# Far passes behind each engine's code, a hinted image loop and an earlier flag load on TensorE

## The chip, the cores and the metric

The kernel runs on one core of a Trainium2 chip. The metric is the device time of one execution in microseconds (us), taken as the median of three runs. A core has engines that run side by side, each with its own stream of instructions: TensorE (PE in the profile; PEld are its weight loads), VectorE (DVE), ScalarE (ACT), GpSimd (POOL) and SyncE (SP, which starts DMA transfers here). Each has a sequencer that reads the stream, waits for semaphores, works on registers and branches; a q behind an engine's name in a row (PEldq, DVEq, ACTq, POOLq) marks work of the sequencer.

## What is computed

Two blocks with residuals on 32 images of 192 channels and 32 x 32 pixels. The first is attention over channels; the second is a 3 x 3 deformable convolution, batch normalization over all images, and gelu.

```python
x = x + _L0_conv_ref(_gn(x), w_qkv, w_out, b_out)
x = x + _L1_conv_ref(_gn(x), proj_w, proj_b, off_w, off_b, mask_w, mask_b, gamma, beta)
...
offset = jnp.clip(_conv(x, off_w, off_b), -max_off, max_off)
mask = 2.0 * jax.nn.sigmoid(_conv(x, mask_w, mask_b))
y = _deform_conv(x, offset, mask, proj_w, proj_b)
mean = y.mean(axis=(0, 2, 3))
var = y.var(axis=(0, 2, 3))
```

`_deform_conv` takes, for each pixel and each of the nine taps, a bilinear sample of the image at a place shifted by `offset`. The offsets depend on the data, so which rows of the image a pixel reads is known only at run time.

## The kernel before

The program is written by hand, engine by engine, with semaphores between the engines; nothing reorders it. An image's convolution is 48 units (`UNITS`). In unit `u` TensorE turns the sampling weights of unit `u + 2` (`turn_s`, L650), multiplies with those of unit `u` (`convolve`, L667 to L669) and makes a piece of the projected image ten units ahead (`z_group`, L636 to L640). ScalarE and VectorE split each result into a high and a low half (L887 and L1142 for the weights, L853 and L1136 for the projected image). GpSimd builds the sampling weights (L1323). The first block of the next image and its offsets are woven into the same 48 units (`part0`). After unit 47 TensorE transposes the last quarter of the output (`turn_y(3)`, L680 and L681), which VectorE scales (`scale_y(3)`, L1204). With the third `turn_s` of the next image's pass, unit 2 of it begins.

The weights made so reach a few rows only, which is enough while all offsets are small. VectorE therefore finds the image's largest offset and writes a flag `far` for each image. TensorE, ScalarE and VectorE each load it into a register (`is_far`, L387 to L389) and branch on it at the image's end (`where_far`): with flag 1 they run a long `far_pass`, otherwise (a near image) they only count up the semaphores that the far pass would have counted. The code of the far pass stands in the stream at this place, in front of the near code, at four places on each of the three engines. On TensorE one such piece is over 2,000 instructions. In the profiled execution no image was far.

`images` runs image 0 by itself, then a loop over images 1 to 30 whose body holds two images, then image 31 by itself. So of the 31 ends of an image that have another image behind them, 15 lie in the middle of the loop's body, 14 are followed by the jump back to the loop's head (the loop's branch has line L346), one leads from image 0 into the loop and one from image 30 out of it. The loop was opened with `eng.Fori`.

After the last image come the statistics of the batch normalization and a stage that loads, normalizes, adds and stores the images in pairs.

Of the kernel before, what the change touches and what calls it, by code (L numbers as in the profile page):

```python
# [82 lines left out]
def build(nc, x, w_qkT, w_v, w_outT, b_out, w_off, b_off, w_proj, proj_b, gamma, beta,  # L83
          avg, cy, cx, eye, out):
    NB = x.shape[0]
# [4 lines left out]
    with ExitStack() as ctx:  # L90
# [6 lines left out]
        def sem(name):  # L97
            return ctx.enter_context(nc.semaphore(name))
# [166 lines left out]
        far_left = sem("far_left")  # L265
# [63 lines left out]
        def all_pairs(eng, step):  # L329
            with eng.Fori(0, ROUNDS) as r_:  # L330
                for i in range(FIN):
                    step(r_, i)
            for i in range(PAIRS - ROUND_ENDS):
                step(ROUNDS, i)

        def images(program, eng):

            part0, part1, weights_ready = program  # L340
            for u in range(SLOTS):
                part0(u, 0, 0)
                if u == 15:
                    weights_ready()
            part1(0, 0, True)
            with eng.Fori(1, NB - 2, 2) as b:  # L346
                part1(b, 1, True)
                part1(b + 1, 0, True)
            part1(NB - 1, (NB - 1) % 2, False)

        far_units = [(t, ky, f) for t in range(TILES) for ky in range(3)
                     for f, c in enumerate(FAR) if 0 <= t + c <= CHUNKS]
        FAR_UNITS = len(far_units)
# [23 lines left out]
        def first(b):  # L378
            return isinstance(b, int) and b == 0
# [5 lines left out]
        def is_far(eng, b, par):  # L385

            eng.wait_ge(flag_sb, b + 1)  # L387
            eng.sem_inc(flag_seen, 1)
            return eng.value_load(far[0:1, par:par + 1], min_val=0, max_val=1)  # L389

        def where_far(flag, eng, b, par, more, far_pass, *counts):

            with eng.If(flag == 1):
                far_pass(b, par, more)
                eng.sem_inc(far_left, 1)
            with eng.Else():
                for s, n in counts:
                    eng.sem_inc(s, n)

        def load_blocks(eng, dst, src, done):  # L400
            eng.dma_start(dst[:, 0], src[0:P]).then_inc(done, 16)
# [81 lines left out]
        def _(pe):  # L483
# [100 lines left out]
            def offset_max(b):  # L584
                pe.wait_ge(omax_sb, b + 1)
                if not first(b):
                    pe.wait_ge(y_ch, 4 * b)
                pe.transpose(yt[:, 0:P], offmax[:, :].broadcast_to([P, P]), eye32[:, :]).then_inc(omax_ps, 1)

            def part0(u, b, par):  # L590
                if u == 4:
                    group_stats(0, b)
                if 12 <= u < 16:
                    transpose_x(u - 12, b)
                if u == 16:
                    gram_product(b)
                if u == 17:
                    gram_times_wq(b)
                if u == 18:
                    pe.wait_ge(t1_sb, b + 1)  # L600
                    square(log_ps, t1, wk, l0[0], C)
                if u == 21:
                    pe.wait_ge(prob_sb, b + 1)
                    square(r_ps, prob, wo, l0[1], C)
                if u == 22:
                    pe.wait_ge(r_sb, b + 1)
                    for m in range(2):
                        o = l0[0][:, m * C:(m + 1) * C]
                        pe.matmul(o, wv[:, 0, m * P:(m + 1) * P], rmat[:, 0], start=True, stop=False)
                        mm = pe.matmul(o, wv[0:CB, 1, m * P:(m + 1) * P], rmat[0:CB, 1], start=False, stop=True)  # L610
                    mm.then_inc(mt_ps, 1)
                if 23 <= u < 27:
                    apply_m(u - 23, b)
                if u == 28:
                    group_stats(1, b)
                if 38 <= u < 40:
                    for t in range(TILES // 2):
                        offset_conv(TILES // 2 * (u - 38) + t, b, par)

            def z_group(g, b, par):  # L620

                if g == 0:
                    pe.wait_ge(x2_moved, b + 1)
                if g >= 2 or not first(b):
                    pe.wait_ge(z_lo, UNITS * b + g - 1)
                z_product(g, par, par).then_inc(z_ps, 1)
# [15 lines left out]
            def turn_s(u, b):  # L642
                t, ky, c = u // 6, u % 6 // 2, u % 2
                if c == 0:
                    pe.wait_ge(st_made, 24 * b + 3 * t + ky + 1)
                if u >= 2 or not first(b):
                    pe.wait_ge(s_lo, UNITS * b + u - 1)
                g = (3 * t + ky) % ST_RING
                for kx in range(3):
                    mm = pe.transpose(sps[u % 2][:, kx * P:(kx + 1) * P], sT[:, g, kx, c * P:(c + 1) * P], eye32[:, :])  # L650
                mm.then_inc(s_ps, 1)

            def convolve(u, b, par):
                i, ky, c = u // 6, u % 6 // 2, u % 2
                pe.wait_ge(s_lo, UNITS * b + u + 1)
                if i + c < CHUNKS and (c == 1 or i == 0):
                    pe.wait_ge(z_lo, UNITS * b + 6 * (i + c) + 2 * ky + 2)
                if u % 6 == 0 and (i > 0 or not first(b)):
                    pe.wait_ge(y_pm, TILES * b + i)
                s_product(u % S_RING, tile_at(i + c, par), ky, u % 6 == 0, u % 6 == 5).then_inc(sz_done, 1)  # L660
# [11 lines left out]
            def turn_y(q, b):  # L672
                pe.wait_ge(y_pm, TILES * b + 2 * q + 2)
                if q == 0:
                    pe.wait_ge(flag_sb, b + 1)
                if q > 0 or not first(b):
                    pe.wait_ge(y_ch, 4 * b + q)
                for i in range(2):
                    y = ypm[:, (2 * q + i) % 4]
                    pe.transpose(yt[:, i * P:(i + 1) * P], y[:, 0:P], eye32[:, :])  # L680
                    mm = pe.transpose(yt[:, (2 + i) * P:(3 + i) * P], y[:, P:2 * P], eye32[:, :])  # L681
                mm.then_inc(yt_ps, 1)
# [45 lines left out]
            def part1(b, par, more):  # L728
                if first(b):
                    for g in range(AHEAD):  # L730
                        z_group(g, b, par)
                    turn_s(0, b)
                    turn_s(1, b)
                for u in range(UNITS):
                    if u + 2 < UNITS:
                        turn_s(u + 2, b)
                    elif more:
                        turn_s(u + 2 - UNITS, b + 1)
                    convolve(u, b, par)
                    if u == 9:  # L740
                        offset_max(b)
                    if u + AHEAD < UNITS:
                        z_group(u + AHEAD, b, par)
                    elif more:
                        z_group(u + AHEAD - UNITS, b + 1, 1 - par)
                    if u % 12 == 2 and u > 12:
                        turn_y(u // 12 - 1, b)
                    if more:
                        part0(u, b + 1, 1 - par)
                flag = is_far(pe, b, par)  # L750
                turn_y(3, b)
                where_far(flag, pe, b, par, more, far_pass, (fz_ps, FAR_Z), (fs_ps, FAR_UNITS), (fsz_done, FAR_UNITS),
                          (fyt_ps, TILES))

            wq, wk = wqk[:, :, 0:C], wqk[:, :, C:2 * C]
            images((part0, part1, weights_ready), pe)

        @block.scalar
        def _(act):  # L760
# [128 lines left out]
            def part1(b, par, more):  # L889
# [27 lines left out]
                where_far(flag, act, b, par, more, far_pass, (fz_hi, FAR_Z), (fs_hi, FAR_UNITS), (fy_pm, TILES))  # L917

            images((part0, part1, lambda: None), act)

# [7 lines left out]
                                   bias=gb[:, m:m + 1]).then_inc(f_gelu, 1)  # L929

            all_pairs(act, gelu_pair)

        @block.vector
        def _(dve):
# [282 lines left out]
            def part1(b, par, more):  # L1218
# [5 lines left out]
                for u in range(UNITS):  # L1224
# [20 lines left out]
                    if more:  # L1245
                        part0(u, b + 1, 1 - par)
                scale_y(3, b, par)
                where_far(flag, dve, b, par, more, far_pass, (fz_lo, FAR_Z), (f_st, 3 * TILES), (fs_lo, FAR_UNITS),
                          (fy_ch, TILES))
                if not more:  # L1250
                    y_stats(2, b, par)
                    y_stats(3, b, par)

            images((part0, part1, weights_ready), dve)

# [15 lines left out]
                    dve.tensor_tensor(fin_y[slot][i], fin_y[slot][i], fin_x[slot][i], ALU.add).then_inc(f_sum, 1)  # L1272

            all_pairs(dve, add_pair)

        @block.gpsimd
# [112 lines left out]
```

## Time and profile before

| what | value |
|---|---|
| median of 3 runs | 4269.75 us (4259.26 to 4272.78) |
| span of the profiled execution | 4284.4 us |
| PE busy | 3630.2 us, 85% |
| DVE busy | 2649.3 us, 62% |
| ACT busy | 2110.5 us, 49% |
| POOL busy | 1410.9 us, 33% |
| mean granted TensorE clock | 0.939 |

The span is the only time that the profile gives for its own execution; it is 14.65 us above the median of the timed runs. A busy share counts the instructions that compute, not the sequencer's. The granted clock is given as a share of full speed: 1.00 is 2.4 GHz and 0.50 is 1.2 GHz. The images take the span up to some 4050 us, the stage of the pairs the rest.

### The profile page before, as it was taken

What the parts mean: (1) busy time and instruction counts of PE and PEld (TensorE: products, weight loads), DVE (VectorE), ACT (ScalarE), POOL (GpSimd) and SP (SyncE); (2) the same over time, 40 slices, a digit from 0 to 9 for tenths busy, and PEclk for the clock granted to TensorE, in tenths of its full rate; (3) what the DMA queues carried; (4) which work ended last, traced back from release to release, by engine and by line L of the source; (5) the groups of instructions that cost most, each with busy time, mean ns of one, the idle gap of its engine ahead of it and who ended that gap; (6) DMA issues with size and microseconds to landing.
All of it is one profiled execution on the core that took longest, in us unless ns stands there. A gap on an engine that the chain in (4) does not pass through costs nothing.

```text
span 4284.4 us, 109949 instructions
## 1 busy us (share of the span) xinstructions
PE 3630.2 (85%) x38338; PEld 3094.4 (72%) x38338; DVE 2649.3 (62%) x5834; ACT 2110.5 (49%) x4790; POOL 1410.9 (33%) x1165
## 2 busy tenths in 40 slices
PE   3999898999989899998989989898998989899700
PEld 2787777877777778777777877777787777778700
DVE  3666666666666666666666666666666666666522
ACT  1555554555455455545545554554555455445432
POOL 1333332333333233333333333333333333333311
PEclk8999999999999999999999999999999999999955
DMA  2000000000000000000000000000000000000298
GB/s 59 18 27 10 28 27 20 27 27 27 10 27 27 20 27 26 27 10 27 27 20 27 26 27 16 21 27 20 27 26 27 21 16 27 27 20 16 60 361 301
DMA packets 50975, 172.85 MB, mean 40 GB/s; under 512 B 9664, under 2 KB 10880, under 8 KB 50176
## 3 DMA queue, kind: packets, MB, share of 16 engines
q1 hardware_dynamic: 39584, 136.75, 10.6%
q0 software_dynamic: 7168, 25.17, 1.5%
q8 instruction: 426, 6.98, 0.7%
q14 instruction: 373, 3.06, 0.2%
q10 hardware_dynamic: 3424, 0.90, 0.1%
HBM read 87.29 MB, written 75.50 MB: 38 GB/s over the span
## 4 chain that ended last, share of the span: by engine, by line
PE 63%; DVE 13%; issue 13%; ACT 4%; DMA 4%; DVEq 1%; ACTq 1%; SPq 1%; POOL 0%; POOLq 0%
PE sps L650 10%; PE acc L667 6%; PE acc L668 6%; PE acc L669 6%; PE l L578 4%; PE zps L636 3%; DVE zl L1136 3%; PE zps L640 3%; PE zps L637 3%; PE zps L638 3%; PE zps L639 3%; DMA xn<-x_scratch 2%; DVE sl L1142 2%; DVE ych L1204 2%; PE l L510 1%
## 5 line engine op out<-in xcount | busy, mean ns | idle before, releaser
L1323 POOL TENSOR_TENSOR sT<-ay,bx 128x768 f32<-128x768 f32 x768 | 1148.1, 1505 | 1615.3 <-PE sps L650 1547.9
L1142 DVE TENSOR_TENSOR sl<-sps,sh 128x384 f16<-128x384 f32 x1536 | 847.1, 552 | 743.7 <-ACT sh L887 740.3
L887 ACT CAST sh<-sps 128x384 f16<-128x384 f32 x1536 | 741.7, 483 | 915.4 <-PE sps L650 905.9
L667 PE MATMUL acc<-zh,sh 128*128 128x192 f16 x4608 | 1155.7, 251 | 0.3 <-ACT ypm L910 0.3
L668 PE MATMUL acc<-zl,sh 128*128 128x192 f16 x4608 | 1155.5, 251 | 0.0
L669 PE MATMUL acc<-zh,sl 128*128 128x192 f16 x4608 | 1155.2, 251 | 0.0
L650 PE MATMUL sps<-eye,sT 128*128 128x128 f32 x4608 | 808.0, 285 | 322.0 <-issue 218.2
L853 ACT CAST zh<-zps 128x288 f16<-128x288 f32 x1536 | 620.1, 404 | 699.6 <-PE zps L640 672.6
L1136 DVE TENSOR_TENSOR zl<-zps,zh 128x288 f16<-128x288 f32 x1536 | 693.9, 452 | 423.0 <-ACT zh L853 415.7
L650 PEld LDWEIGHTS sps<-eye,sT 128*128 128x128 f32 x4608 | 544.5, 143 | 451.9 <-issue 229.4
L667 PEld LDWEIGHTS acc<-zh,sh 128*128 128x128 f16 x4608 | 459.0, 100 | 37.5 <-issue 35.9
L668 PEld LDWEIGHTS acc<-zl,sh 128*128 128x128 f16 x4608 | 459.1, 100 | 20.9
L669 PEld LDWEIGHTS acc<-zh,sl 128*128 128x128 f16 x4608 | 459.1, 100 | 1.6
L636 PE MATMUL zps<-wpr_h,x_hi_a 128*128 128x288 f16 x1344 | 392.1, 292 | 0.8 <-DVE zl L1136 0.3
L637 PE MATMUL zps<-wpr_l,x_hi_a 128*128 128x288 f16 x1344 | 390.8, 291 | 0.0
L638 PE MATMUL zps<-wpr_h,x_lo_a 128*128 128x288 f16 x1344 | 390.1, 290 | 0.0
L639 PE MATMUL zps<-wpr_h,x_hilo_b 128*128 128x288 f16 x1344 | 389.7, 290 | 0.0
L640 PE MATMUL zps<-wpr_l,x_hilo_b 128*128 128x288 f16 x1344 | 389.7, 290 | 0.0
L1307 POOL TENSOR_TENSOR bx<-off,cx_sb 128x576 f32<-128x576 f32 x128 | 155.3, 1213 | 459.4 <-DVE off L1103 459.4
L1289 POOL TENSOR_TENSOR rstd<-gvar,mhalf 128x2 f32<-128x2 f32 x64 | 44.8, 700 | 582.0 <-DVE gvar L993 582.0
L578 PE MATMUL l<-wof,x2s_hi_a 128*128 128x54 f16 x1536 | 183.0, 186 | 9.8 <-DVE x2w_hilo_b L1009 9.8
L578 PE MATMUL l<-wof,x2s_lo_a 128*128 128x54 f16 x1536 | 182.8, 186 | 0.0
(200 smaller groups left out, 6498.0 us busy)
## 6 DMA issues: line engine op xcount, KB each, us to landing
xin<-in_x SPq DMA_DIRECT2D x32, 512.0 KB, 5.5
xin<-in_x SPq DMA_DIRECT2D x64, 256.0 KB, 5.9
x_scratch<-x SPq DMA_DIRECT2D x32, 512.0 KB, 2.8
y_scratch<-ych SPq DMA_DIRECT2D x32, 512.0 KB, 2.7
zh<-y_scratch SPq DMA_DIRECT2D x20, 512.0 KB, 11.0
zl<-x_scratch SPq DMA_DIRECT2D x20, 512.0 KB, 12.0
out<-zh POOLq DMA_DIRECT2D x20, 512.0 KB, 8.8
x_scratch<-x SPq DMA_DIRECT2D x32, 256.0 KB, 3.5
```

The source lines that it names most:

```text
L578: mm = pe.matmul(o, src[:, row * W:(row + ROWS_T) * W], wof[:, m, k].rearrange("p i j -> p (i j)"), start=(k == 0 and n == 0), stop=(k == ...
L636: pe.matmul(o, at(0), wpr_h[:, 0, ky, n], start=True, stop=False)
L637: pe.matmul(o, at(0), wpr_l[:, 0, ky, n], start=False, stop=False)
L650: mm = pe.transpose(sps[u % 2][:, kx * P:(kx + 1) * P], sT[:, g, kx, c * P:(c + 1) * P], eye32[:, :])
L667: pe.matmul(acc[:, 0:C], s_h, zh[:, j, ky, z], start=start and kx == 0, stop=False)
L668: pe.matmul(acc[:, 0:C], s_h, zl[:, j, ky, z], start=False, stop=False)
L669: mm = pe.matmul(acc[:, 0:C], s_l, zh[:, j, ky, z], start=False, stop=stop and kx == 2)
L853: act.copy(z_piece(zh, g, par), zps[:, g % 2, 0:KO // 2]).then_inc(z_hi, 1)
L887: act.copy(sh[:, u % S_RING].rearrange("p k n -> p (k n)"), sps[u % 2][:, 0:3 * P]).then_inc(s_hi, 1)
L1136: dve.tensor_tensor(z_piece(zl, g, par), zps[:, g % 2, 0:KO // 2], z_piece(zh, g, par), ALU.subtract)\
L1142: dve.tensor_tensor(one(sl), sps[u % 2][:, 0:3 * P], one(sh), ALU.subtract).then_inc(s_lo, 1)
L1323: pool.tensor_tensor(sT[:, p % ST_RING].rearrange("p k (r x) -> p k r x", r=R), a, x_, ALU.mult)\
```

## The change

It has four parts.

- TensorE loads the flag after unit 20's `convolve`, where before it did so behind unit 47.
- Nothing else is moved, and all instructions that compute stay.

```diff
-            with eng.Fori(1, NB - 2, 2) as b:
+            with nc.Fori(1, NB - 2, 2, engines=bass.OrderedEngineSet([eng.engine]), hint_back_edge=True) as b:
...
         def where_far(flag, eng, b, par, more, far_pass, *counts):
 
-            with eng.If(flag == 1):
-                far_pass(b, par, more)
-                eng.sem_inc(far_left, 1)
-            with eng.Else():
-                for s, n in counts:
-                    eng.sem_inc(s, n)
+            k = len(far_bodies)
+            name = f"{eng.engine.name}_{k}"
+            origin = nc.cur_bb
+            eng.br_cond(flag == 1, f"far_{name}", f"near_{name}")
+            nc.switch_bb(f"near_{name}")
+            for s, n in counts:
+                eng.sem_inc(s, n)
+            eng.br(f"joined_{name}")
+            nc.switch_bb(f"joined_{name}", parent=origin)
+            far_bodies.append((name, origin, far_pass, b, par, more))
+
+        def far_code(eng):
+
+            eng.br(f"done_{eng.engine.name}")
+            for name, origin, far_pass, b, par, more in far_bodies:
+                with nc.body(f"far_{name}", parent=origin, valid_engines=[eng.engine]):
+                    far_pass(b, par, more)
+                    eng.sem_inc(far_left, 1)
+                    eng.br(f"joined_{name}")
+            far_bodies.clear()
+            nc.switch_bb(f"done_{eng.engine.name}")
...
                     if u == 9:
                         offset_max(b)
+                    if u == 20:
+                        flag = is_far(pe, b, par)
...
-                flag = is_far(pe, b, par)
                 turn_y(3, b)
...
             images((part0, part1, weights_ready), pe)
+            far_code(pe)
```

On TensorE, at the image's end in the middle of the loop's body, the branch is followed by the far pass before the change (ISA rows are register work and waits, plain semaphore counts are not rows):

```order
L387 REGISTER_ALU
L389 TENSOR_LOAD far
L389 ISA x2
L673 ISA
L677 ISA
L680 MATMUL yt<-eye,ypm 128x128
L681 MATMUL yt<-eye,ypm 128x128
L680 MATMUL yt<-eye,ypm 128x128
L681 MATMUL yt<-eye,ypm 128x128
L393 COMPARE_AND_BRANCH
L685 ISA
```

Over 1,100 rows of far pass later the near code and the next image follow:

```order
L393 UNCONDITIONAL_BRANCH
L396 UNCONDITIONAL_BRANCH
L645 ISA
L647 ISA
L650 MATMUL sps<-eye,sT 128x128 x3
```

After the change the same place reads (all line numbers behind `where_far` are 16 higher here):

```order
L696 MATMUL yt<-eye,ypm 128x128
L697 MATMUL yt<-eye,ypm 128x128
L397 COMPARE_AND_BRANCH
L401 UNCONDITIONAL_BRANCH
L661 ISA
L663 ISA
L666 MATMUL sps<-eye,sT 128x128 x3
```

The far pass and the flag's load are gone from here, and the next image's first `turn_s` stands behind the branch.

On TensorE, at the loop's head, there is one new instruction after the change:

```order
L346 UNCONDITIONAL_BRANCH
L346 BRANCH_PREFETCH_HINT
L346 ISA
L663 ISA
L666 MATMUL sps<-eye,sT 128x128 x3
```

At the loop's end the closing branch now stands two rows behind the flag's branch:

```order
L397 COMPARE_AND_BRANCH
L401 UNCONDITIONAL_BRANCH
L346 REGISTER_ALU
L346 COMPARE_AND_BRANCH
L666 MATMUL sps<-eye,sT 128x128 x3
```

Before, a far pass stood between the two compare-and-branch rows as well.

## Rows read from the trace of the kernel before

**Rows 1.** The page's first part: busy us (share of the span) and instructions.

```profile
PE 3630.2 (85%) x38338; PEld 3094.4 (72%) x38338; DVE 2649.3 (62%) x5834; ACT 2110.5 (49%) x4790; POOL 1410.9 (33%) x1165
```

**Rows 2.** Waits: engine, line, what it waited for: total us, times, longest us.

```profile
PE sps L650 <- issue: 218.2, 46, 8.8
```

**Rows 3.** Timeline of PE, image 1 to 2: start us, us, instruction [idle before].

```profile
361.53 0.68 PE L650 MATMUL sps<-eye,sT 128*128 128x128 f32 x2 [4.34 <-issue]
363.99 0.37 PE L650 MATMUL sps<-eye,sT 128*128 128x128 f32 x1 [1.78 <-issue]
...
369.23 0.49 PE L650 MATMUL sps<-eye,sT 128*128 128x128 f32 x3
...
370.91 0.49 PE L650 MATMUL sps<-eye,sT 128*128 128x128 f32 x3
```

**Rows 4.** Timeline of PE, image 2 to 3, over the loop's jump back.

```profile
488.87 0.90 PE L650 MATMUL sps<-eye,sT 128*128 128x128 f32 x3 [8.53 <-issue]
...
495.00 0.49 PE L650 MATMUL sps<-eye,sT 128*128 128x128 f32 x3
```

**Rows 5.** Timeline of PE, image 0 to 1, then image 30 to 31.

```profile
239.91 0.90 PE L650 MATMUL sps<-eye,sT 128*128 128x128 f32 x3 [4.36 <-issue]
...
245.93 0.49 PE L650 MATMUL sps<-eye,sT 128*128 128x128 f32 x3
...
3972.48 0.73 PE L650 MATMUL sps<-eye,sT 128*128 128x128 f32 x3 [4.25 <-issue]
...
3977.54 0.49 PE L650 MATMUL sps<-eye,sT 128*128 128x128 f32 x3
```

**Rows 6.** Branches by line: count, ns min/median/max, first and last start us.

```profile
L393 PEldq COMPARE_BRANCH  x32: 3435/3771/4165, 234.9 to 4050.7; - x32
...
L346 PEldq COMPARE_BRANCH  x15: 79/4355/4657, 484.3 to 3972.2; - x15
...
L346 POOLq COMPARE_BRANCH  x15: 40/45/50, 469.0 to 3956.8; - x15
```

**Rows 7.** The same view, 354 to 364 us: flag's branch, near code, next image's first instruction.

```profile
L393 PEldq COMPARE_BRANCH  x1: 4022/4022/4022, 356.6 to 356.6; - x1
...
L398 DVEq EVENT_SEMAPHORE  x4: 21/21/21, 360.3 to 360.6; - x4
L398 PEldq EVENT_SEMAPHORE  x4: 51/51/51, 360.7 to 361.2; - x4
...
L645 PEldq FUSED_REGOPS  x1: 51/51/51, 361.3 to 361.3; - x1
```

**Rows 8.** Stretches: us; busy us (instructions) by engine; PEclk, DMA share, GB/s.

```profile
361.40:368.20 6.80, 4.89 (x24) 3.87 (x25) 1.14 (x3) 1.17 (x3) 0.34 (x1) 0.50 0.01 2
368.20:480.00 111.80, 107.62 (x1175) 92.25 (x1174) 76.71 (x174) 62.71 (x146) 41.60 (x34) 1.00 0.09 25
```

**Rows 9.** Timeline of DVE around the same end of image 1.

```profile
358.61 0.98 DVE L1204 TENSOR_SCALAR ych<-yt,unscale,pb 128x256 f32<-128x256 f32 x2
...
370.84 0.54 DVE L1142 TENSOR_TENSOR sl<-sps,sh 128x384 f16<-128x384 f32 x1
371.55 0.46 DVE L1136 TENSOR_TENSOR zl<-zps,zh 128x288 f16<-128x288 f32 x1 [0.17 <-ACT zh L853]
371.92 1.28 DVE L974 BATCH_NORM_STATS2 stats<-xin 128x6 f32<-128x512 f32 x2
...
374.00 0.56 DVE L1142 TENSOR_TENSOR sl<-sps,sh 128x384 f16<-128x384 f32 x1
```

**Rows 10.** Before and behind the flag's load; L680 by form (busy us, mean ns | idle); inside image 2.

```profile
L387 PEldq ALU_OP  x1: 32/32/32, 354.5 to 354.5; - x1
...
L673 PEldq FUSED_REGOPS  x1: 37/37/37, 355.5 to 355.5; - x1
...
L680 PE MATMUL yt<-eye,ypm 128*128 128x128 f32 x256 | 64.5, 279 | 2.9 <-ACT ypm L910 0.5
...
450.02 0.55 PE L650 MATMUL sps<-eye,sT 128*128 128x128 f32 x3 [1.08 <-DVE sl L1142]
```

**Rows 11.** Timeline of DVE behind the last image.

```profile
4054.82 1.28 DVE L1214 BATCH_NORM_STATS2 ystats<-ych 128x6 f32<-128x512 f32 x2 [2.42 <-DVEq L398]
```

## Prediction made before the run

> **What bounds the kernel.** I read the page's busy times first: TensorE is busy for 85% of the span, no other engine for more than 62% [rows 1]. So for the images, which fill nearly all of the span, TensorE's stream sets the pace, and what counts is when it stands still. The view of the waits names one large loss on it: before line L650, which is the turning of the sampling weights, it sat idle for 218.2 us in 46 stretches, and the releaser is "issue": no engine and no DMA was late [rows 2]. The timeline shows where. Each stretch lies at an image's end, behind the last L681. From image 1 to 2, in the middle of the loop's body, PE waits 4.34 us, runs two transposes, and waits another 1.78 us [rows 3]. Over the loop's jump back it waits 8.53 us [rows 4]. Out of image 0 and out of image 30 it waits 4.36 and 4.25 us [rows 5]. The count agrees: 14 ends at 8.5, 17 at 4.25 and 15 second waits of 1.8 make 46 stretches and 119 + 72 + 27 = 218 us.
>
> The sequencer's rows say what it is. The branch on the flag took 3.4 to 4.2 us in all 32 images, always jumping over the far pass to the near code [rows 6]. The loop's branch took 4.36 us at the median, and 79 ns in the one case where it was not taken, at the loop's exit [rows 6]. A jump to code that is far off costs some 4 us, a branch that goes straight on almost nothing. GpSimd's loop branch is taken too, but its body is some 140 instructions, and it took 45 ns [rows 6].
>
> There is a second loss behind each wait. The granted clock is 1.00 in the image (2.4 GHz), and falls to 0.50 (1.2 GHz) for the 6.8 us that follow the wait of image 1 [rows 8]. Since each pause costs twice, I don't add up branches, but measure the whole stretch from the end of the last L681 to the third group of L650, where unit 2 of the next image begins. In full run a unit takes 370.91 - 369.23 = 1.68 us [rows 3], so two units need 3.37 us.
>
> - Middle of the body: 369.23 - (361.53 - 4.34) = 12.04 us [rows 3], 8.67 too long, 15 times.
> - Jump back: 495.00 - (488.87 - 8.53) = 14.66 us [rows 4], 11.29 too long, 14 times.
> - Image 0: 245.93 - 235.55 = 10.38 us; image 30: 3977.54 - 3968.23 = 9.31 us [rows 5]; 7.01 and 5.94 too long.
>
> All of it is 130.1 + 158.1 + 13.0 = 301 us. That is the most that the change can give in the images.
>
> **The change, part by part.**
>
> The branch on the flag. For a near image it is no longer taken, so the nearest row is the loop's exit, 79 ns instead of 3.77 us [rows 6]. The four semaphore counts of the near code stay. They run from 360.7 to 361.2, and the next image's first instruction stands at 361.3 [rows 7]: 0.6 us, and 0.2 more until its first transpose at 361.53 [rows 3]. The branch starts at 356.6 [rows 7], 0.6 us before the last transpose of `turn_y` ends at 357.19, which covers most of it. 0.1 + 0.6 + 0.2 - 0.6 is 0.3, so I take 0.3 us of idle time for PE in the middle of the body. The second wait of 1.78 us, which has the same cause (code behind a jump that isn't there yet), goes too, since nothing is jumped to. The stretch becomes 0.3 + 3.37 = 3.67 us and the gain 12.04 - 3.67 = 8.37 us, 15 times: 125.6 us. Image 30 gains 9.31 - 3.8 = 5.5, and image 0, with a register move and the hint besides, 10.38 - 4.0 = 6.4.
>
> VectorE and ScalarE. VectorE's near code started at 360.3 [rows 7], though its last operation had ended at 359.59 [rows 9]: it pays such a jump too, covered so far by TensorE's longer wait, and loses it in the same way. What is late next is VectorE: it ends `scale_y(3)` at 358.61 + 0.98 = 359.59 us, 2.4 us behind TensorE's last transpose [rows 9]. Then it has for units 0 to 2 a split of the weights, a split of the projected image and a statistic each, then one more statistic and the moments, before TensorE's group sums behind unit 4. A weight split takes 0.54 us, an image split holds the next back by 0.37 (371.55 to 371.92), a statistic adds 0.60 (two take 1.28), and the moments take 0.8, from 373.20 to 374.00 [rows 9]: 3 x 1.51 + 0.6 + 0.8 = 5.9 us, so ready at 365.5. TensorE would be there at 357.19 + 0.3 + 5 x 1.68 = 365.9. It just fits, with 0.4 us to spare, so no loss in the sum, but I allow 0.2 us at each of 31 ends: 6 us back.
>
> The clock. If PE idles for 0.3 to 0.75 us, does it still fall? Inside image 2 PE waits 1.08 us at 450 us [rows 10], and the clock stays at 1.00 from 368.2 to 480 [rows 8]. So I expect no fall, and its share (about 2.5 us at each end, contained in the stretches above) is gained. Its price if it falls nonetheless: 31 x 2.5 = 78 us.
>
> The flag's load in mid-image. The load and the register work around it take TensorE's sequencer from 354.5 to 355.5, about 0.9 us [rows 10]. At the old place the array hardly noticed: the idle time before all 256 transposes of L680, which stand behind it, is 2.9 us [rows 10], since the sequencer works ahead of the array. Ahead of unit 20's `z_group` the mix of instructions is the same, so I cost it at nothing; without that cover it is 0.9 x 32 = 29 us. The flag itself is written in VectorE's unit 11, nine units or 15 us earlier.
>
> The far code behind the rest. At the end each of three engines takes one jump over it, 4 us, when its work is done and the last stores are under way: nothing. VectorE's last branch does lie on the path: its statistics waited 2.42 us [rows 11] for the near code. Gain 2.3 us.
>
> Sum: 125.6 + 147.6 + 6.4 + 5.5 + 2.3 - 6 = 281 us. The profiled span of 4284.4 would become 4003; against the median of 4269.75, 3989 us. Since a run without the profiler may save a little more or less, I put 3990.
>
> **The rivals.**
>
> The hint does nothing (**A**). The jump back still costs one fetch. The nearest row is image 0's end, one jump and the clock behind it, 10.38 us [rows 5]. Each jump back then gains 4.3 instead of 10.54 us, 87 us less in all: 4077 us. For it speaks that the target lies two images of instructions back and that no row shows a hint at work.
> The Trainium skill (Runtime: NRT & Kernel Launch, Instruction fetch mechanics) says that a taken branch whose target is outside the two pages at hand forces a DMA fetch before execution goes on, and names no way round it; the 4.36 us of the loop's branch and GpSimd's 45 ns both agree with that rule. By it the time would be this rival's.
>
> VectorE becomes the bound at the ends (**B**). If the moments or the splits come 1 to 2 us late, through ScalarE's latency or a jump back that VectorE still pays, 31 x 1.5 = 47 us come back: 4036 us. The clock would stay up.
>
> The clock falls in spite of short pauses (**C**): 78 us back, 4068 us.
>
> Slower (**D**): the near code is still jumped to, and its closing branch (L401, unconditional) is a second jump of 3.8 us with 0.5 us more at the low clock. Then each of 31 ends costs 4.3 us more, 133 us, and the hint gives back 14 x 4.3 = 60: 4343 us. It decides on whether a branch to the next address costs a fetch. Against it: the old near code ended in such a branch too (L396), and its last semaphore count and the next instruction stand 0.15 us apart, like the counts among themselves; and the loop's branch has the same form, straight on if false, at 79 ns.
>
> **Chances.** The forecast 0.72; A 0.12; B 0.08; C 0.04; D 0.04. The forecast by itself spans 3968 (nothing of the 301 us stays) to 4018 (the load's 29 us are seen). The range goes from 3968 to 4050, so that B is in; A, C and D are left out, 0.20. This kernel's measurement can tell about 0.3% from no change. Faster by more 0.96, which is the forecast, A, B and C; slower 0.03, and within it 0.01, which share D, since its jumps could cost less where the target is at hand.
>
> **What would show it.** In the changed profile the flag's branch should have some 0.08 us on PE; the loop's branch under 0.5 us; the "issue" wait before `turn_s` should fall from 218 us to under 25; the stretch from the last transpose to unit 2 should be about 3.7 us in the body and 4.1 over the jump; and the granted clock should stay at 1.00 through the images. A loop branch of 4.3 us means A. Waits of `turn_s` or the group sums for VectorE at the ends mean B. A gap in the middle of unit 20 means that the load is not covered. The forecast is wrong if the pauses vanish and the span doesn't follow.

## The result and the profile after

The changed kernel took 3995.86 us (median of 4 runs, 3991.55 to 4003.37), against 4268.81 us before (4 runs here, one more than in the table above): a ratio of 0.9371, 95% interval 0.9349 to 0.9393, or 273 us less. The forecast was 3990 us. The profiled execution had a span of 3992.2 us, 292 us less than the one of before.

The page's first part and its row of the granted clock in 40 slices of the span:

```profile
PE 3544.1 (89%) x38338; PEld 3034.8 (76%) x38338; DVE 2646.4 (66%) x5834; ACT 2111.3 (53%) x4790; POOL 1412.8 (35%) x1165
...
PEclk8999999999999999999999999999999999999955
```

TensorE runs the same 38338 matmuls, but is busy for 86 us less than in [rows 1]. Nothing of its work was taken away, so this is the clock: matmuls at 1.2 GHz last longer. From 120 to 3770 us, which is all of the images but the start of image 0 and the last 2.7 us, the granted clock is 1.00 throughout (columns as in [rows 8]):

```profile
120.00:3770.00 3650.00, 3495.59 (x37896) 3002.51 (x37896) 2540.09 (x5679) 2024.78 (x4694) 1356.28 (x1077) 1.00 0.08 24
```

The same stretch of the kernel before, to 4048 us:

```profile
120.00:4048.00 3928.00, 3579.39 (x37890) 3060.33 (x37889) 2542.46 (x5678) 2023.67 (x4695) 1354.48 (x1077) 0.97 0.08 23
```

The branches on the flag (now L397) and of the loop (L346) on TensorE, columns as in [rows 6]:

```profile
L397 PEldq COMPARE_BRANCH  x32: 71/86/91, 234.7 to 3772.1; - x32
...
L346 PEldq COMPARE_BRANCH  x15: 80/377/404, 465.7 to 3693.4; - x15
```

The flag's branch costs 86 ns instead of 3.77 us (medians). The loop's branch costs 0.38 us instead of 4.36, and 80 ns where it isn't taken.

Of the 218.2 us of waits before `turn_s` in [rows 2] this is left; the first row holds most of the short waits at the images' ends (engine, line, what it waited for: total us, times, longest us):

```profile
PE sps L666 <- POOL sT L1343: 17.3, 23, 1.0
...
PE sps L666 <- issue: 2.7, 8, 0.3
```

That the old waits were for code to be fetched is borne out by the DMA queue that brings TensorE's instructions (queue, kind: packets, MB, share of the 16 DMA engines). Before, then after:

```profile
q8 instruction: 426, 6.98, 0.7%
```

```profile
q8 instruction: 337, 5.52, 0.6%
```

These are packets of 16 KB. In the 13 us around each image's end in the middle of the body (from 1 us ahead of the last transpose's end to 12 us behind it) there were three of them before, and there is one now. The queue is TensorE's: when only the code of ScalarE and VectorE differs (the layout on TensorE alone, below), this row stays at 337, and the other instruction queue, q14, goes from 209 to 347 packets.

The timeline of PE from image 1 to 2, to be held against [rows 3]; L666 is the old L650, and the third row of it opens unit 2:

```profile
350.79 0.54 PE L666 MATMUL sps<-eye,sT 128*128 128x128 f32 x3 [0.33 <-issue]
352.52 0.49 PE L666 MATMUL sps<-eye,sT 128*128 128x128 f32 x3
354.20 0.49 PE L666 MATMUL sps<-eye,sT 128*128 128x128 f32 x3
```

The stretch is 354.20 - 350.46 = 3.74 us, where it was 12.04. Over the jump back from image 2 to 3, against [rows 4]:

```profile
466.47 0.54 PE L666 MATMUL sps<-eye,sT 128*128 128x128 f32 x3 [0.99 <-POOL sT L1343]
...
469.90 0.49 PE L666 MATMUL sps<-eye,sT 128*128 128x128 f32 x3
```

It is 469.90 - 465.48 = 4.42 us, where it was 14.66. The releaser that this row names, GpSimd's weights, is only the semaphore that the instruction looks at. The 0.99 us are filled by the sequencer's own work: the four counts, the counter, 0.40 us of loop branch, the hint and two register instructions stand one behind the other from 465.0 to 466.4.

VectorE behind the last image, against [rows 11]:

```profile
3772.76 0.99 DVE L1223 TENSOR_SCALAR ych<-yt,unscale,pb 128x256 f32<-128x256 f32 x2 [2.34 <-PE yt L697]
3773.78 1.29 DVE L1233 BATCH_NORM_STATS2 ystats<-ych 128x6 f32<-128x512 f32 x2
```

Its statistics follow without the 2.42 us.

The end of the last image's transposes shows how the gain is split. Before and after:

```profile
4051.09 0.27 PE L681 MATMUL yt<-eye,ypm 128*128 128x128 f32 x1
```

```profile
3772.44 0.27 PE L697 MATMUL yt<-eye,ypm 128*128 128x128 f32 x1
```

The images gave 278.65 us. The rest of the span, 233.0 us before and 219.5 after, gave 13.5 more, of which the statistics explain 2.4. The remaining 11 us belong to no edit: the stage of the pairs waits for DMA transfers, and with the same code it lasted from 213.9 to 235.8 us in the profiles of four kernels below that end alike. This is also why the timed runs differ by 273 us where the two profiles differ by 292. For parts worth a few microseconds I therefore read the images' end in the profile, not the total.

### The profile page after: what moved, and what is told of

It is laid out like the page before. It is cut to its first block, busy times and chain, and to the rows that moved or that the text cites. A ratio compares the mean times of both kernels' runs of the same rounds, so it can differ in the third digit from the quotient of the medians.

```text
span 3992.2 us, 110012 instructions
## 1 busy us (share of the span) xinstructions
PE 3544.1 (89%) x38338; PEld 3034.8 (76%) x38338; DVE 2646.4 (66%) x5834; ACT 2111.3 (53%) x4790; POOL 1412.8 (35%) x1165
## 4 chain that ended last, share of the span: by engine, by line
PE 66%; DVE 12%; issue 9%; DMA 4%; POOL 3%; ACT 3%; DVEq 1%; SPq 1%; ACTq 0%; POOLq 0%
PE sps L666 10%; PE acc L683 6%; PE acc L685 6%; PE acc L684 6%; PE l L594 4%; PE zps L652 3%; PE zps L656 3%; PE zps L653 3%; PE zps L655 3%; PE zps L654 3%; DVE zl L1155 3%; DMA xn<-x_scratch 2%; POOL sT L1343 2%; DVE sl L1161 2%; PE l L526 2%
## 5 line engine op out<-in xcount | busy, mean ns | idle before, releaser
L683 PE MATMUL acc<-zh,sh 128*128 128x192 f16 x4608 | 1133.7, 246 | 0.9 <-issue 0.6
L685 PE MATMUL acc<-zh,sl 128*128 128x192 f16 x4608 | 1133.6, 246 | 0.0
L684 PE MATMUL acc<-zl,sh 128*128 128x192 f16 x4608 | 1133.6, 246 | 0.0
L666 PE MATMUL sps<-eye,sT 128*128 128x128 f32 x4608 | 785.8, 279 | 127.2 <-DVE sl L1161 99.4
L666 PEld LDWEIGHTS sps<-eye,sT 128*128 128x128 f32 x4608 | 530.9, 140 | 283.5 <-DVE sl L1161 167.9
L684 PEld LDWEIGHTS acc<-zl,sh 128*128 128x128 f16 x4608 | 450.9, 98 | 17.7 <-issue 0.8
L683 PEld LDWEIGHTS acc<-zh,sh 128*128 128x128 f16 x4608 | 450.8, 98 | 2.4 <-DVE sl L1161 0.5
L685 PEld LDWEIGHTS acc<-zh,sl 128*128 128x128 f16 x4608 | 450.9, 98 | 0.0
```

The lines of the kernel that those rows point to most:

```text
L683: pe.matmul(acc[:, 0:C], s_h, zh[:, j, ky, z], start=start and kx == 0, stop=False)
L684: pe.matmul(acc[:, 0:C], s_h, zl[:, j, ky, z], start=False, stop=False)
L685: mm = pe.matmul(acc[:, 0:C], s_l, zh[:, j, ky, z], start=False, stop=stop and kx == 2)
```

## The experiments

In each timeline below the stretch is measured as in the prediction: from the end of an image's last transpose to unit 2 of the next.

**Without the hint.** The changed kernel, far code behind the rest, no hint.

```diff
-            with nc.Fori(1, NB - 2, 2, engines=bass.OrderedEngineSet([eng.engine]), hint_back_edge=True) as b:
+            with nc.Fori(1, NB - 2, 2, engines=bass.OrderedEngineSet([eng.engine]), hint_back_edge=False) as b:
```

> The changed kernel without the hint on the loop's closing branch; far code stays behind the rest. If the prediction's account of the jump is right (rival A's price), each of the 14 jumps back costs one fetch again: the loop's branch on TensorE takes some 4.3 us, the stretch from the last transpose to unit 2 is some 10.4 us there (3.8 in the body's middle, unchanged), the clock falls behind those 14 alone, and the time is 84 to 88 us above the changed kernel: about 4082 us. If the hint did little and the gain was all in the layout, the time stays within 10 us of 3996.

Measured: 4071.65 us, ratio 0.9526 to the kernel before (0.9507 to 0.9545); against 0.9371 for the change, 66 us more by the two ratios; the images end at 3839.59 us, 67 us later. The loop's branch, the jump back from image 2 to 3, the clock behind it, and TensorE's instruction queue:

```profile
L346 PEldq COMPARE_BRANCH  x15: 67/3649/3829, 464.8 to 3762.1; - x15
```

```profile
468.56 0.55 PE L666 MATMUL sps<-eye,sT 128*128 128x128 f32 x3 [3.97 <-issue]
...
473.64 0.49 PE L666 MATMUL sps<-eye,sT 128*128 128x128 f32 x3
```

```profile
469.50:472.90 3.40, 3.40 (x21) 2.91 (x19) 1.77 (x4) 1.08 (x3) 0.96 (x1) 0.50 0.00 0
```

```profile
q8 instruction: 350, 5.73, 0.6%
```

The jump costs one fetch again, 3.65 us at the median, with 13 packets of code more than in the changed kernel, and the clock falls behind all 14 of these jumps and nowhere else from 120 us to the images' end. So layout and hint are both real: rival A's mechanism exists, and the hint removes it. The stretch is 473.64 - 464.59 = 9.05 us here (9.42 on average over the 14), not 10.4, so the hint's share is 14 x 5.0 = 70 us and not 87. The jump is 0.7 us cheaper than the one of before, and the clock stays low for 3.4 us behind eight of the jumps, where it was 6.8 behind image 0, which I had taken as the nearest row; behind the other six it is 6.8 here too.

The images' end moved by 67 us and not 70 in part because of a wait behind the loop's exit. In the changed kernel TensorE waits in unit 1 of image 31:

```profile
3696.92 0.24 PE L683 MATMUL acc<-zh,sh 128*128 128x192 f16 x1 [0.60 <-issue]
```

Without the hint this wait is absent, and the stretch behind image 30 is 3.83 us instead of 4.62. In the kernels below that have both layout and hint it is 0.87 to 2.91 us, but for the one with 26 counts, which has none. Whether the hint itself or the place of the code makes it was not taken apart.

**The hint alone.** The kernel before, with the hint as the one edit.

```diff
-            with eng.Fori(1, NB - 2, 2) as b:
+            with nc.Fori(1, NB - 2, 2, engines=bass.OrderedEngineSet([eng.engine]), hint_back_edge=True) as b:
```

> The kernel before with the hint alone. Theory: the sequencer fetches the hinted target when it enters the block of code that holds the closing branch. Here it enters that block by the jump to the near code, some 0.7 us ahead of the closing branch, so the fetch has hardly begun: the loop's branch drops from 4.36 to some 3 us at best, and 14 x 1 = 14 us are gained: about 4255 us. Rival (parts add up): the hint is worth the 84 to 88 us by itself, or at least 14 x 4.3 = 60 us: 4209 us or less.

Measured: 4240.25 us, ratio 0.9924 (0.9905 to 0.9943), about 32 us less; in the profile the images end 46 us earlier, at 4005.62 us. The loop's branch and the jump back:

```profile
L346 PEldq COMPARE_BRANCH  x15: 89/2682/2906, 481.2 to 3926.1; - x15
```

```profile
484.45 0.90 PE L650 MATMUL sps<-eye,sT 128*128 128x128 f32 x3 [6.91 <-issue]
```

Read at the images' end, the same hint is worth 67 us with the far code away and 46 us without. Of the 46, the jumps back have 14 x 2.68 = 38 us, 1.63 us of idle time and 1.05 us of the clock each. Most of the rest lies at the ends in the middle of the body, 0.6 us each, where nothing was edited. The loop's branch is 1.67 us shorter, more than the 1.0 to 1.4 I had put, and far from the 0.38 of the changed kernel. This agrees in kind with what I expected, that the hint needs time between the arrival at the code near the loop's end and the branch: here the sequencer gets there by a jump, 0.7 us ahead (near code from 480.5, loop branch at 481.2). But that the fetch starts on entering a block of code is my reading; it wasn't measured by itself. The amount was missed: it lies between the 14 us of the theory and the 60 of the rival.

**Far code that is never run, made longer.** The kernel before, TensorE only.

```diff
             def far_pass(b, par, more):
+                if par == 1 and more:
+                    for _ in range(64):
+                        pe.sem_inc(far_left, 1)
                 pe.wait_ge(s_lo, UNITS * (b + 1) + 2 * more)
```

> The kernel before with 64 semaphore counts added to TensorE's far pass of the body's first image, which is never run: it only moves the near code and the images behind it by 64 places. Theory: the second wait of 1.8 us behind 15 of the jumps comes from the near code standing some ten places before the end of a block of fetched code. Moved by 64 it stands near a block's start, the second wait is gone, the stretch falls from 12.0 to some 10.4 us, 15 times: 24 us less, about 4245 us. Rival: the second wait is for data (GpSimd's or VectorE's) and stays: 4269 us.

Measured: 4223.87 us, ratio 0.989 (0.9869 to 0.9911): 49 us less, from 64 instructions that no image executes. Image 1 to 2:

```profile
360.96 0.68 PE L650 MATMUL sps<-eye,sT 128*128 128x128 f32 x3 [3.79 <-issue]
...
366.04 0.49 PE L650 MATMUL sps<-eye,sT 128*128 128x128 f32 x3
```

```profile
361.20:364.60 3.40, 3.40 (x20) 2.90 (x19) 0.56 (x1) 0.76 (x2) 0.00 (x0) 0.50 0.00 0
```

```profile
q8 instruction: 411, 6.73, 0.7%
```

The three transposes now run together; the second wait of 1.78 us of [rows 3] (1.5 to 2.3 over the 15 ends) is gone at all 15, and with it 15 of the 426 packets of code. So it was a wait for another piece of code, not one for data. That the jump had landed near the end of what was fetched is my reading of it; the run shows that the place of the code decides. The stretch is 366.04 - 357.17 = 8.87 us (9.03 on average), not the 10.4 that I expected: the clock came back after 3.4 us instead of 6.8. Of the 51 us at the images' end, the middle of the body has 15 x 2.96 = 44, and the jumps back, whose code has moved as well, 6. Two neighbouring kernels thus differ by 1% through nothing but where their code lies.

**Pauses without a jump.** The changed kernel with 13, then 26 more counts of 0.15 us in TensorE's near code.

```diff
             for s, n in counts:
                 eng.sem_inc(s, n)
+            for _ in range(13 if eng is nc.tensor else 0):
+                eng.sem_inc(paused, 1)
             eng.br(f"joined_{name}")
```

> The changed kernel with 13 more semaphore counts (0.15 us each) in TensorE's near code: a pause of 2.0 us more at each image's end, with no jump. It measures what a pause costs by itself. Theory: the granted clock falls by the pause's length and not because code is fetched; with 2.3 us idle in the body's middle and 2.9 us at the jump back it stays up, as it does over the 1.08 us inside an image: 31 x 2.0 = 61 us more, 4057 us. If pauses this short bring it down too, some 2 to 2.7 us more at each end: 4120 to 4140 us.

> The same with 26 counts: 3.9 us more, so 4.3 us idle in the body's middle, as long as the old jump to the near code, and 4.9 us at the jump back. Theory: the pause alone brings the clock to 0.50 behind each end, as in the kernel before: 31 x 3.93 = 122 us for the pauses and 31 x (1.6 to 2.65) = 50 to 82 us for the clock: 4168 to 4200 us. Rival: the clock's fall belongs to the fetch of far code, and a plain pause leaves it at 1.00: 4118 us.

Measured: 4097.6 us with 13 (ratio 0.9604, 0.9573 to 0.9634) and 4208.05 us with 26 (0.9863, 0.9813 to 0.9912); 102 and 212 us above the changed kernel's 3995.86; the images end 102 and 195 us later than its 3772.72. The clock with 13 counts behind image 1, where it falls, and behind image 3, where it doesn't; then behind images 0, 1 and 2 with 26:

```profile
358.90:362.30 3.40, 3.40 (x21) 2.91 (x20) 1.68 (x4) 1.13 (x3) 0.87 (x1) 0.51 0.02 5
594.00:605.00 11.00, 9.04 (x90) 8.45 (x90) 8.63 (x22) 5.08 (x11) 2.60 (x2) 1.00 0.01 2
```

```profile
239.60:246.40 6.80, 5.08 (x27) 4.46 (x28) 1.64 (x4) 1.36 (x3) 0.83 (x1) 0.50 0.00 0
362.50:365.90 3.40, 3.26 (x17) 2.77 (x18) 0.56 (x1) 0.48 (x1) 0.00 (x0) 0.51 0.00 0
481.90:488.70 6.80, 2.97 (x16) 2.56 (x17) 0.56 (x1) 0.48 (x1) 0.00 (x0) 0.50 0.02 5
```

The pause alone brings the clock down; no fetched code is needed. The rival is out. My own expectation for the short pause is out too: with 13 counts the clock falls behind 22 of the 31 ends. These are all 16 with 2.5 to 3.0 us of idle time (14 jumps back, image 0 and image 30) and 6 of the 15 in the body's middle, which idle for 2.3 to 2.4 us. Of the 102 us some 62 are idle time at the ends and 40 the rest, most of it the clock. With 26 counts the clock falls behind all 31. Of the 195 us, 132 are idle time at the ends, 10 more than the 122 of the counts, and 62 are left for the clock, 2.0 us at each end. The 10 come mostly from the loop's branch, which had a median of 0.47 us there but up to 2.14, with 14 packets of code more than in the changed kernel (351 against 337). So 26 places of code ahead of it are enough to take part of the hint's effect away; why was not taken apart. The rest of the 212 us lies behind the images, in the stage of the pairs.

**The layout on TensorE alone.** The changed kernel, with ScalarE and VectorE back at the old form.

```diff
         def where_far(flag, eng, b, par, more, far_pass, *counts):
 
+            if eng is not nc.tensor:
+                with eng.If(flag == 1):
+                    far_pass(b, par, more)
+                    eng.sem_inc(far_left, 1)
+                with eng.Else():
+                    for s, n in counts:
+                        eng.sem_inc(s, n)
+                return
             k = len(far_bodies)
```

> The changed kernel with the far code moved on TensorE alone; ScalarE and VectorE keep it in front of the near code, as before. If TensorE's jump is all that mattered, the time is that of the changed kernel, 3996 us. If VectorE's jump is next in line (it held VectorE some 0.7 us beyond its last operation, and VectorE had 0.4 us to spare by the prediction's sum, with ScalarE's split behind its own jump 2.4 us after TensorE's last transpose), each of 31 ends is 0.3 to 2 us longer: 4005 to 4058 us, and TensorE waits at the ends for VectorE or ScalarE.

Measured: 4051.52 us, ratio 0.9471 (0.9441 to 0.9501); by the two ratios 43 us above the change, by the images' end (3818.57 us) 46. The jump back from image 2 to 3: TensorE's wait, ScalarE's and VectorE's first splits, and their loop branch and loop head:

```profile
473.68 0.55 PE L674 MATMUL sps<-eye,sT 128*128 128x128 f32 x3 [1.77 <-DVE sl L1168]
```

```profile
472.04 0.48 ACT L913 CAST sh<-sps 128x384 f16<-128x384 f32 x1 [5.01 <-PE acc L693]
```

```profile
473.07 0.56 DVE L1168 TENSOR_TENSOR sl<-sps,sh 128x384 f16<-128x384 f32 x1 [3.37 <-ACT sh L913]
```

```profile
L346 ACTq COMPARE_BRANCH  x1: 69/69/69, 469.9 to 469.9; - x1
...
L346 ACTq BRANCH_PREFETCH_HINT  x1: 35/35/35, 471.8 to 471.8; - x1
...
L346 DVEq BRANCH_PREFETCH_HINT  x1: 58/58/58, 472.9 to 472.9; - x1
```

So the jumps of the two other engines matter as soon as TensorE's is gone. Both jump to the near code, reach the loop's end late, as TensorE does in the kernel with the hint alone, and pay again until 471.8 and 472.9. TensorE then waits for them. Of the 46 us by the images' end: an image behind a jump back takes 2.7 us longer (14 times, 38 us), one behind an end in the body's middle 0.4 us (15 times, 6 us). On these two engines the branch's own row is short although it is taken; what the jump costs is the time until the engine's next row. Here is ScalarE at the end of image 1 in the kernel before, 3.0 us:

```profile
L393 ACTq COMPARE_BRANCH  x1: 54/54/54, 356.5 to 356.5; - x1
```

```profile
L398 ACTq EVENT_SEMAPHORE  x3: 17/17/17, 359.5 to 359.7; - x3
```

**The hint on TensorE alone.**

```diff
-            with nc.Fori(1, NB - 2, 2, engines=bass.OrderedEngineSet([eng.engine]), hint_back_edge=True) as b:
+            with nc.Fori(1, NB - 2, 2, engines=bass.OrderedEngineSet([eng.engine]), hint_back_edge=eng is nc.tensor) as b:
```

> The changed kernel with the loop's hint on TensorE alone; ScalarE, VectorE and GpSimd jump back without one. VectorE's and ScalarE's bodies are longer than what is fetched ahead, GpSimd's is not. Theory: VectorE's fetch of some 3 us starts while it still works off 1.8 us of queued operations, so it starts the next image 1.2 to 1.5 us later, which uses up its 0.4 us to spare: 14 x (0.1 to 1.1), 2 to 15 us more: 3998 to 4011 us. Rival (TensorE alone matters at the jump back): 3996 us. Other rival (as in the kernel with the layout on TensorE alone, where jumps back were 2.0 to 2.7 us longer): 28 to 38 us more, 4024 to 4034 us.

Measured: 3990.94 us, ratio 0.9366 (0.9337 to 0.9394), no clear difference from the change, 0.9371; in the same series the changed kernel itself had 4004.80 us and 0.9382. VectorE behind the jump back, and its branch and loop head:

```profile
468.69 0.56 DVE L1161 TENSOR_TENSOR sl<-sps,sh 128x384 f16<-128x384 f32 x1 [1.21 <-ACT sh L905]
```

```profile
L346 DVEq COMPARE_BRANCH  x1: 67/67/67, 465.7 to 465.7; - x1
...
L346 DVEq FUSED_REGOPS  x1: 63/63/63, 468.6 to 468.6; - x1
```

VectorE does pay 2.9 us for its jump, of which 1.21 show as idle time, and TensorE doesn't feel it: the images end at 3772.26 us, against 3772.72. I had 2 to 15 us here. The 0.4 us to spare was reckoned with VectorE working through without a pause, but in the changed kernel it waits for ScalarE in each of these units anyway, 0.54, 0.17 and 0.17 us behind image 2, and can give that up. One jump on these engines is covered or nearly so (0.4 us at each end in the middle of the body, in the kernel with the layout on TensorE alone), two are not.

**The flag's load at its old place.**

```diff
-                    if u == 20:
-                        flag = is_far(pe, b, par)
...
+                flag = is_far(pe, b, par)
                 turn_y(3, b)
```

> The changed kernel with TensorE's flag load at its old place, behind unit 47. Theory: the load lies in the sequencer's lead over the array at either place, so it makes no difference: 3996 us, within 5 us, and no new idle time before the last transposes. Rival: now that the jump is gone, the 0.9 us of register work at the image's end are seen, 31 x 0.9 = 28 us: 4024 us.

Measured: 4007.29 us, ratio 0.9378 (0.9349 to 0.9406), beside 4004.80 us and 0.9382 (0.9356 to 0.9409) for the changed kernel in the same series:

> The changed kernel once more, on the chip of the three kernels beside it, as their reference: 3996 us by both theories, within 0.2%.

That repeat came out 0.2% above its first result, with the images ending at 3774.05 us. With the late load they end at 3774.9. The edit is worth nothing that can be seen, at either place.

**A better order.** The branch on the flag and the four counts stand ahead of the last four transposes; the far code makes these transposes itself.

```diff
             for s, n in counts:
                 eng.sem_inc(s, n)
+            both()
             eng.br(f"joined_{name}")
...
-                turn_y(3, b)
                 where_far(flag, pe, b, par, more, far_pass, (fz_ps, FAR_Z), (fs_ps, FAR_UNITS), (fsz_done, FAR_UNITS),
-                          (fyt_ps, TILES))
+                          (fyt_ps, TILES), both=lambda: turn_y(3, b))
```

> The changed kernel with TensorE's branch on the flag and the near code's four semaphore counts ahead of the last four transposes of the image, not behind them. The changed kernel still idles 0.36 us (body's middle) and 0.96 us (jump back) on TensorE at an image's end, and the four counts take 0.6 us of its sequencer. Theory: TensorE's sequencer is the bound there, the counts now stand in its wait for ScalarE's copy of the sums, and up to 15 x 0.36 + 14 x 0.6 = 14 us go: 3982 to 3988 us. Rival: VectorE, with 0.4 us to spare by the prediction, is late next and takes the gain back: 3992 us or more.

Measured: 3977.76 us (3976.09 to 3988.53), ratio 0.9328 (0.9301 to 0.9355), 27 us below the changed kernel in its series; the images end at 3755.1 us, 18 to 19 below. The rest of the 27 is the spread of the last stage. Image 1 to 2 and the jump back behind image 2:

```profile
351.84 0.27 PE L699 MATMUL yt<-eye,ypm 128*128 128x128 f32 x1
351.95 0.49 PE L668 MATMUL sps<-eye,sT 128*128 128x128 f32 x3
```

```profile
466.83 0.54 PE L668 MATMUL sps<-eye,sT 128*128 128x128 f32 x3 [0.23 <-issue]
```

In the body's middle no idle time is left, and over the jump 0.23 us. The gain of 18 to 19 us is a little more than my 14, since the transposes of the two images also overlap by 0.16 us. This kernel beats both. It uses the early load: the flag has to be in its register before the branch.

## Why the prediction was right

**The reading of the idle time** held. The 218 us of "issue" were jumps, and they went with the jumps and with 89 packets of code. The stretches came out as follows, per end, with the prediction's value in brackets: body's middle 3.74 to 3.86 us (3.67), jump back 4.40 (4.12), image 0 4.04 (4.0), image 30 4.62 (3.8). The images gave 278.65 us in the profile, where the terms without the 2.3 us of the statistics come to 279. That the two agree to within 1 us is in part luck: the ends gave 2.4 us less in the body's middle, 2.4 less over the jumps back and 0.8 less behind image 30 than their terms, and the 6 us set aside for VectorE were not needed.

**The term for the loop's branch** was a little low: 0.38 us for a taken branch with a hint, where I had reckoned with GpSimd's 0.05 and 0.3. It made each stretch 0.28 us longer than forecast, 4 us in all, of which 1.5 came back because the stretches before were 14.77 us on average and not 14.66. GpSimd's row was also weaker support than I took it for: ScalarE and VectorE show taken branches of 0.05 to 0.07 us as well, and yet stood for some 3 us behind them. What counts is the 0.3 us until GpSimd's next instruction. Behind image 30 the stretch was 0.8 us too long through the wait of 0.60 us in unit 1 of image 31, which I hadn't seen coming; it is missing in the kernel without the hint.

**The clock** stayed up over 0.3 to 1 us of idle time, as forecast from the 1.08 us of [rows 10]. The pauses show how little room there was: 2.3 to 2.4 us was already too long at 6 of 15 ends. The price per end, "about 2.5 us", is right only for the kernel before, where it was 2.65 on average; in the other kernels whose clock falls it was 1.8 to 2.1 on average. Rival C, priced with it at 78 us, would by those have cost some 60, an estimate.

**The second wait** behind the jump was given to missing code without proof; the longer far code shows it. The rule that I cited from the Trainium skill (Runtime: NRT & Kernel Launch, Instruction fetch mechanics), that a taken branch whose target is outside the two pages at hand forces a fetch, agrees with TensorE's unhinted jumps here, medians of 3.65 to 4.36 us with their packets of code. It names no way round the wait and so led me to rival A; the measurement decides: with the hint the taken branch has 0.38 us.

**Slower (rival D)** is out: the near code's closing branch (L401) costs nothing that shows, since TensorE waits for 0.33 to 0.44 us in all between two images in the body's middle.

**VectorE as next in line** was right in kind: with its and ScalarE's old jumps kept, 46 us of the gain are gone. That they were needed had no term in my sum, since their edits come together with TensorE's; on its own, TensorE's edit would have missed the forecast. That VectorE just fits was right in result and wrong in size: it idles for 1.21 us behind an unhinted jump back and TensorE doesn't feel it. The price of rival A, 87 us, was too high; it is 67 to 70.

**The flag's load** costs nothing, as costed. **The end** of the program, with one jump over the far code on three engines, shows no cost that stands out of the spread of the last stage. The total of 3995.86 is 6 us above 3990; by the profile's stages that is within the spread of the last stage.

## What to carry to other kernels

When an engine idles with "issue" as the reason, look at its branches: code that is rarely run belongs behind the rest, so that the common path is not a jump, and it must move on every engine that takes part. A loop longer than what is fetched ahead wants a hint on its closing branch, and on the evidence of two kernels its worth depends on the code before that branch: when that was reached by a jump the branch took 2.68 us instead of 0.38, and 26 more instructions there cost part of it again. Count such a pause twice: the idle time, and the TensorE clock behind it.

## What the runs showed of the hardware

- A jump to far code costs TensorE 3.4 to 4.7 us ([rows 6]) and VectorE and ScalarE some 3 us (2.9 in the kernel with the hint on TensorE alone, 3.0 before); not taken, TensorE's branch costs 0.08 us; taken with the hint, in the changed kernel, 0.38 us.
- Where a jump lands decides whether a second wait of 1.5 to 2.3 us for one more packet of code follows. 64 instructions that never ran, put in front, took it away at 15 ends and made the kernel 1.1% faster (ratio 0.989).
- The clock falls to 1.2 GHz after a plain pause of TensorE as it does after a fetch. It fell behind all 31 pauses of 4.3 to 6.8 us (26 counts), behind all 16 of 2.5 to 3.0 us and 6 of 15 of 2.3 to 2.4 us (13 counts). With the layout on TensorE alone it fell behind its two longest waits at a jump back, 2.1 us, and not behind twelve of 1.6 to 1.9 us. In the changed kernel's images, with waits of up to 1.2 us, it did not fall.
